# State-space layer's scan: out product ahead of the block products, ScalarE's exponentials and copies in another order

## What is computed

```python
proj = hidden_states @ in_proj_w * mup
z, xBC, dt = proj[..., :512], proj[..., 512:1280], proj[..., 1280:]
xBC = silu(causal_conv4(xBC) + conv_b)
x, B, C = xBC[..., :512], xBC[..., 512:640], xBC[..., 640:]
dt = softplus(dt + dt_bias); dA = exp(-exp(A_log) * dt); dtx = dt[..., None] * x
def step(state, inp):                    # over the tokens
    dA_t, dtx_t, B_t, C_t = inp
    state = state * dA_t + outer(dtx_t, B_t)
    return state, einsum(C_t, state)
y = ys + D * x
yn = y * rsqrt(mean(y ** 2) + 1e-5) * norm_w
out = (yn * silu(z)) @ out_proj_w        # added to the residual stream
```

## Time and profile before

| | us |
|---|---|
| median of 3 runs | 590.24 |
| lowest, highest | 589.28, 593.54 |
| the profiled execution | 590.71 |
| its span, first to last instruction | 589.0 |
| in it: the scan, first XB to last x_res | 265.2 to 475.5 |

### The profile page before, as it was taken

One profiled execution on the slowest core, in us unless ns is written; L12 is line 12 of the kernel. 1 busy time (PEld: TensorE's weight loads), 2 busy tenths in 40 slices (PEclk: granted clock), 3 DMA queues, 4 the chain that ended last, 5 costly groups with the idle time before them and its releaser, 6 DMA issues. The chain is left out here.

```text
span 589.0 us, 17155 instructions
## 1 busy us (share of the span) xinstructions
PE 493.7 (84%) x7504; PEld 413.5 (70%) x7504; DVE 391.1 (66%) x758; ACT 282.6 (48%) x506; POOL 176.3 (30%) x213
## 2 busy tenths in 40 slices
PE   4879897999969797737889788988788549999997
PEld 3657696988948675635777677766676438988986
DVE  6968837365579997955688666787657635464642
ACT  2665624252346779745655465555636113242331
POOL 1100006021066100255566654666636310000000
PEclk9989998999999899768999988999879958999999
DMA  9920060000000000020000000000430000101011
GB/s 204 264 107 0 26 278 1 1 1 1 1 1 0 2 0 1 0 55 2 7 3 4 3 4 5 4 3 5 162 147 3 3 1 0 37 0 37 2 36 37
DMA packets 7162, 21.33 MB, mean 36 GB/s; under 512 B 688, under 2 KB 5296, under 8 KB 6448
## 3 DMA queue, kind: packets, MB, share of 16 engines
q1 hardware_dynamic: 6688, 18.08, 9.2%
q10 hardware_dynamic: 400, 2.16, 1.6%
HBM read 12.90 MB, written 6.55 MB: 33 GB/s over the span
## 5 line engine op out<-in xcount | busy, mean ns | idle before, releaser
L433 POOL TENSOR_TENSOR n_rstd<-n_ve,m_half 128x4 f32<-128x4 f32 x12 | 13.2, 1101 | 208.1 <-DVE n_ve L429 208.1
L1162 POOL TENSOR_TENSOR w<-xdt,ends 32x512 f32<-32x512 f32 (+1 forms) x64 | 67.1, 1072 | 2.7 <-PE prior L977 2.5
L1060 DVE TENSOR_TENSOR mmat<-seg,gs 128x512 f32<-128x512 f32 x64 | 42.5, 684 | 35.8 <-ACT seg L1015 35.8
L733 DVE SCALAR_TENSOR_TENSOR cv<-pre,vec,cv 128x512 f32<-128x512 f32 x72 | 59.6, 843 | 3.5 <-ACT cv L787 2.6
L66 PE MATMUL f_down<-wd,f_hT 128*128 128x256 f32 x192 | 54.9, 286 | 2.1 <-ACT wd L283 1.6
L1045 ACT ACTIVATE xbd<-xdt 32x512 f32<-32x512 f32 x64 | 40.2, 628 | 29.1 <-PE intra L992 27.9
L68 PE MATMUL f_down<-wd,f_hT 128*128 128x256 f32 x192 | 54.0, 281 | 0.0
L67 PE MATMUL f_down<-wd,f_hT 128*128 128x256 f32 x192 | 54.0, 281 | 0.0
L1015 ACT ACTIVATE seg<-seg 128x512 f32<-128x512 f32 x64 | 36.9, 578 | 35.0 <-PE seg L936 35.0
L66 PE MATMUL f_gate<-n_xT,wgu 128*128 128x512 f32 x96 | 39.7, 413 | 7.7 <-DVE f_h L235 3.1
L936 PEld LDWEIGHTS seg<-abk,m_seg 96*32 96x32 bf16 x2048 | 20.6, 97 | 28.5 <-DVE mmat L1060 15.4
(11 more groups left out here) (181 smaller groups left out, 1283.4 us busy)
## 6 DMA issues: line engine op xcount, KB each, us to landing
wgu_dram<-wgu SPq DMA_DIRECT2D x1, 2816.0 KB, 8.2
wgu<-wgu_dram SPq DMA_DIRECT2D x1, 2816.0 KB, 10.5
out<-x_res SPq DMA_DIRECT2D x4, 512.0 KB, 2.9
x_res<-in_x SPq DMA_DIRECT2D x1, 1536.0 KB, 24.3
wd_dram<-wd SPq DMA_DIRECT2D x1, 1536.0 KB, 11.5
wd<-wd_dram SPq DMA_DIRECT2D x1, 1536.0 KB, 14.0
gu_idx<-in_gu ACTq DMA_DIRECT2D x4, 352.0 KB, 8.1
gu_idx<-in_gu SPq DMA_DIRECT2D x4, 352.0 KB, 12.8
```

The costliest lines, as they stand in the source:

```text
L433: pool.tensor_tensor(self.rstd[:, :], self.ve[:, :], self.T["m_half"][:, 0:GT], ALU.pow).then_inc(self.rstd_ok, 1)
L733: dve.scalar_tensor_tensor(dst, pre[:, x, k:k + GN].rearrange("p (t c) -> p t c", c=P), cw[:, x, k:k + 1], dst, ALU.mult, ALU.add).then_in ...
L1060: dve.tensor_tensor(mmat[a % 2][:, i, :], seg[u_ % 2][:, :, :], gs[a % 2][:, i].unsqueeze(2).broadcast_to([P, IU, HEADS]), ALU.mult).then_ ...
L1162: pool.tensor_tensor(heads(w[r, n, :]), heads(xdt[a % 2][r, :]), ends[a % 2][r, n * HEADS:(n + 1) * HEADS].unsqueeze(2) .broadcast_to([Q * ...
```

## The change

On TensorE the out product of stage z moves from the end of the step to behind unit 3, ahead of `intra` and unit 4. On VectorE x_res moves ahead of the addition of `intra` to `y`. On ScalarE exponential 2 moves ahead of sq, the copies to xbd are made in the next step (the first at its head, ahead of bg, the other three behind uh), and exponential 4 ends the step, behind ve_y. On GpSimd `w` is cut in two: two blocks ahead of rstd_y and two behind it. No arithmetic changes.

```diff
@@ TensorE, behind segments(a, 3)
+                if do_z:
+                    wait(pe, "yf_ok", 4 * (z + 1))
+                    wait(pe, "red_ok", z + 1)
+                    pe.matmul(yo[:, HID:HID + 1], ssum[:, 0, :], T["ones"][:, 0:1], start=True, stop=True)
+                    wait(pe, "uhi_ok", z + 1)
+                    wait(pe, "ulo_ok", z + 1)
+                    for k in range(4):
+                        ins = split_mm(pe, yo[:, 0:HID], uh[:, 0, k, :], uh[:, 1, k, :], wout[:, 0, k, :],
+                                       wout[:, 1, k, :], k == 0, k == 3)
+                    ins.then_inc(s["out_ok"], 1)
                 if do_b:
                     wait(pe, "m_ok", (UNITS - 1) * (b_ + 1))
                     wait(pe, "xbd_ok", NB * (b_ + 1))
...
@@ ScalarE
+            def blocks_of_x(b_, first, last):
+                wait(act, "xdt_ok", b_ + 1)
+                wait(act, "intra_ok", b_)
+                for b in range(first, last):
+                    r = slice(Q * b, Q * b + Q)
+                    act.activation(xbd[r, :, b, :], heads(xdt[b_ % 2][r, :]), ACT.Copy).then_inc(s["xbd_ok"], 1)
+
             for a, b_, z, do_a, do_b, do_z in steps():
+                if do_b:
+                    blocks_of_x(b_, 0, 1)
                 if do_a:
...
                     decays(a, 0)
                     decays(a, 1)
+                    decays(a, 2)
                 if do_z:
...
-                if do_a:
-                    decays(a, 2)
+                if do_b:
+                    blocks_of_x(b_, 1, NB)
+                if do_a:
                     decays(a, 3)
-                    wait(act, "xdt_ok", a + 1)
-                    wait(act, "intra_ok", a)
-                    for b in range(NB):
-                        r = slice(Q * b, Q * b + Q)
-                        act.activation(xbd[r, :, b, :], heads(xdt[a % 2][r, :]), ACT.Copy).then_inc(s["xbd_ok"], 1)
-                    decays(a, 4)
                 if do_z:
                     wait(act, "out_ok", z + 1)
                     wait(act, "rs_ok", z)
...
+                if do_a:
+                    decays(a, 4)
@@ VectorE, behind masked(a, 3)
+                if do_z:
+                    wait(dve, "out_ok", z + 1)
+                    wait(dve, "rs_ok", z + 1)
+                    dve.scalar_tensor_tensor(x_res[:, z, :], yo[:, 0:HID], rstd[:, 0:1], x_res[:, z, :], ALU.mult,
+                                             ALU.add).then_inc(s["res_ok"], 1)
@@ GpSimd, weighted(a, n) is the old body of the loop over n
+                    weighted(a, 0)
+                    weighted(a, 1)
                 if do_z:
                     wait(pool, "ve_ok", z + 1)
                     wait(pool, "res_ok", z)
                     pool.tensor_tensor(rstd[:, :], ve[:, :], T["m_half"][:, 0:1], ALU.pow).then_inc(s["rs_ok"], 1)
+                if do_a:
+                    weighted(a, 2)
+                    weighted(a, 3)
```

More of the change, by code:

```diff
@@ L996, in _ @@
                     segments(a, 4)
[L997 to L1006, removed]
         @block.scalar
@@ L1126, in _, with weighted @@
                     masked(a, 4)
[L1127 to L1131, removed]
         @block.gpsimd
         def _(pool):
+            def weighted(a, n):
+                wait(pool, "exp_ok", a * UNITS + 1)
+                wait(pool, "xdt_ok", a + 1)
+                wait(pool, "prior_ok" if n < NB - 1 else "new_ok", a)
+                r = slice(0, Q * (n + 1))
+                pool.tensor_tensor(heads(w[r, n, :]), heads(xdt[a % 2][r, :]),
+                                   ends[a % 2][r, n * HEADS:(n + 1) * HEADS].unsqueeze(2)
+                                   .broadcast_to([Q * (n + 1), HEADS, PD]), ALU.mult).then_inc(s["w_ok"], 1)
             pool.memset(eps[:, :], EPS).then_inc(s["set_ok"], 1)
```

## The result

The changed kernel takes 573.24 us (median of 4 runs, 571.96 to 575.54), the kernel before 591.16 us in the same comparison: ratio 0.973, 95% interval 0.969 to 0.977. The forecast was 581.2 us with a range from 573.0 to 588.5: the direction and the range held, the size forecast was about half of what came. The profiled execution spans 572.5 us against 589.0, 16.5 us less.

The account below looks back on a forecast made before the run. A loop of dependences, with no engine full, set the step. Loop 9.6 + fill 1.9 + drain 0.5 - stalls 3.0 = 9.0 us off 590.71 gave 581.7, less 0.47: 581.2 us, range 573 to 588.5.

Parts of the forecast that it names:

- The loop: Undisturbed scan step, transposes to next transposes: from 11.04 to 10.3 us including hand-overs, times 13, 9.6 us gained.
- The three late copies: ScalarE's xbd copies behind uh end ahead of intra's start, with 1.0 us of cover: cost nothing.
- y: VectorE's addition of intra, 0.64 us, fits ahead of the next transposes with 1 us of cover: costs nothing.
- rstd_y: On GpSimd between second and third w: two w outlast out by at most some tenths, cost nothing.
- exponential 3: On ScalarE behind the three copies, near 5.4 us, ahead of end sums some 3.5 us later: costs nothing.
- The fill: Steps 0 and 1: exponential 4 could start where the copies did, TensorE waiting less: 1.9 us gained.
- The drain: Scan's end, from step 15's x_res to the last: 0.5 us gained, bounds -1.5 and +1.5.
- the weight I gave to step 15's copies: In the scan's end, step 15 leaves its copies and exponential 4 earlier, counted as 2.5 us in favour.
- Instruction stalls: TensorE's stalls with reason "issue" in the scan: two more of 1.5 us, 3 us lost.
- the dense parts move together: On TensorE intra, segments 4 and next segments lie closer, formerly parted by out and a 1.23 us wait: 3 us lost.
- Rival A: All of the scan's gain lands, no further stall, fill gives 3.5 us: 576.6 us, chance 0.26.
- B: Shorter scan steps stall more, mean period stays near 12.45 us, only fill and drain remain: 588 us, chance 0.22.

Follow-up runs that it names:

- e1: Kernel before with only TensorE's and VectorE's new lists, ScalarE's and GpSimd's old: 632.3 us, ratio 1.083 to the kernel before.
- e2: Kernel before with only ScalarE's new list, the other engines' lists old: 591.4 us, ratio 1.011 to the kernel before.
- e4: Changed kernel with GpSimd's old list, all four w in one piece ahead of rstd_y: 573.7 us, ratio 0.979 to the kernel before.
- e8: Changed kernel with VectorE's old list, x_res behind the addition of y and mmat 4: 575.1 us, ratio 0.977 to the kernel before.
- e13: Changed kernel with half of the segment matmuls left out and GpSimd's w in one piece: 564.9 us, ratio 0.960 to the kernel before.
- e6: Changed kernel with each segment matmul issued twice: 626.2 us, ratio 1.062 to the kernel before.

## Why the prediction was right, and where its sizes were off

**The mechanism.** The wait of the transposes for x_res is gone, so is that of xbd for intra, the undisturbed period is the sum of TensorE's list and one chain back to the third segments, and TensorE waits for mmat there. e1 and e2 show that neither TensorE's nor ScalarE's list does it alone, e4 and e8 that GpSimd's and VectorE's add little in the full kernel.

**The loop, 9.6 us.** The sum's terms came out nearly one by one: transposes to third segments 395.87 - 391.76 = 4.11 (4.12 forecast), third segments 0.35 (0.35), out with the switch of weights 398.06 - 396.22 = 1.84 (1.91), and the rest from intra on by the difference to 10.17, 3.87 (3.83). What failed was the addition of 0.09 us "for hand-overs": they were in the rows already. And the gain holds over 14 periods from one transposes start to the next, not 13. 14 x (11.04 - 10.17) = 12.2 us, 2.6 more than forecast. (The changed kernel once more has a shortest period of 10.25, which would make it 11.1.)

**The three late copies, y, rstd_y, exponential 3: nothing.** Right. The copies ended at 396.9, 1.2 us ahead of intra, for a cover of 1.0 forecast. rstd_y's place is worth 0.6 us of an undisturbed period (e4, e13), had w not been cut in two.

**The fill, 1.9 us.** 2.95 measured. The exponentials 4 no longer hold TensorE, and the denser stretch stalled once, for 1.51 us: between the bounds, for the reason given.

**The drain, 0.5 us gained.** 1.95 us lost, beyond my bound of -1.5. (The forecast counted from the x_res of step 15. Counted so, 4.2 us are lost, 22.24 against 18.05; of these 2.2 lie between that x_res and the transposes of step 16, where a stall of 1.54 us stood.) The step that failed is the weight I gave to step 15's copies. They gave nothing, because counted from the transposes of step 16 they are over. What remained is the 2 us that I named: intra, at 447.88, and y lie between the out product and the last transposes, which had to wait 0.81 us for y:

```profile
439.87 0.66 PE L960 MATMUL yo<-ident,y 128*128 128x128 f32 x4
...
447.88 2.07 PE L1002 MATMUL intra<-xbd,mmat 128*32 128x32 f32 x128
...
450.76 0.66 PE L960 MATMUL yo<-ident,y 128*128 128x128 f32 x4 [0.81 <-DVE y L1135]
```

More than half of the 1.95 us is the clock, which the forecast did not have in its drain. The twelve matmuls of out come behind a wait of 0.93 us; they start 0.21 us apart and take 2.7 us (granted clock 0.68 from 443.88 to 447.88), where those of the kernel before start 0.12 apart and take 1.5 (granted clock 1.00). In the changed kernel's other trace they take 1.6 us, and its drain is 18.40 us long: 1.0 lost, within the bounds.

```profile
445.19 0.41 PE L66 MATMUL yo<-wout,uh 128*128 128x256 f32 x1 [0.93 <-POOL uh L1169]
445.40 0.41 PE L67 MATMUL yo<-wout,uh 128*128 128x256 f32 x1
```

**Instruction stalls, 3 us lost.** This had the wrong sign: the excess of the 14 periods over the undisturbed ones is 173.63 - 14 x 11.04 = 19.1 us before and 158.81 - 14 x 10.17 = 16.4 us now, 2.7 us gained. The step that failed is "the dense parts move together", from which I made two stalls more: in the 13 periods the stalls became more but shorter, 18 with 12.5 us in all instead of 12 with 15.9. Less time ran at the lower clock (0.95 to 0.99 in the 13 periods). The count of instructions is equal (36 and 37 packets). In the kernel before, the transposes stood their 1.2 us for x_res in four of the eight periods with a long stall as well, so a stall there came on top of the loop. What part of the 2.7 us is that and what is the clock was not tried apart, and a part can be chance: the changed kernel's other trace has 159.90 us for its 14 periods, 1.1 more, and the kernel before has one trace only.

Sum: 12.2 + 2.95 - 1.95 + 2.7 + 0.7 behind the scan = 16.6 us against 16.5 of span, where 9.0 were forecast. So the range held because it was wide enough for three terms of the sum that were too low by 1 to 6 us and one too high by 2.5; the forecast's own band, 579 to 584.3 us, was missed. Rival A came nearest with 576.6 us; its reason, that all of the loop's gain lands, was right. B was wrong, though its mechanism exists: it takes back most of changes of 0.4 to 0.6 us per period (e4, e8), not 0.87 on a kernel whose mean lay a microsecond higher. The Trainium skill's page "Runtime: NRT & Kernel Launch", "Instruction fetch mechanics", has 256 instructions to a 16 KiB block, with which e6's 13 packets for 13 x 256 instructions agree. That the fetch is mostly hidden doesn't hold for this scan: without half of the segment matmuls 11 of 16 us of excess went.

## What to carry to other kernels

Where several engines wait for one another in a loop, sum the loop through all in-order lists before moving anything: one side changed alone can make it longer by a third (e1), and yet be needed for the gain. Take the durations from starts in an undisturbed step, and add nothing for hand-overs that such rows contain. And where the stream of small matmuls is dense, compare two periods, the shortest and the mean: what separates them here goes with the number of instructions per time, and it can swallow an improvement of the loop (e4) that shows at once when the instructions are fewer (e13).

## What the runs showed of the hardware

The instruction queue brings 256 instructions per packet, and in none of the 14 traces did two of its packets for TensorE start less than 3.27 us apart, not even where TensorE stood idle for want of them; e6 came to 3.82 us on the mean. A packet's landing and the end of the stall that waited for it lie 1.2 to 1.6 us apart, in 140 stalls of 140. 128 segment matmuls more per step cost 3.3 us per period (14.69 - 11.42), of which 1.7 are TensorE's busy time and 1.6 stalls. The longest stall of every trace belongs to a packet that started while the weights were loading. Why packets keep their distance is open; nothing was tried on it.
